# Attention scores and maxima as pairs of 64-row matmuls, and each projection as one run of twelve

## What is computed

```python
q, k, v = (proj(Wq), proj(Wk), proj(Wv))
scores = jnp.einsum('bhqd,bhkd->bhqk', q, k)
bias = rel_bias[_relative_position_buckets(S)]
scores = scores + bias.transpose(2, 0, 1)[None]
attn = jax.nn.softmax(scores, axis=-1)
ctx = jnp.einsum('bhqk,bhkd->bhqd', attn, v)
```

## Time and profile before

| | |
|---|---|
| median of 3 runs | 3967.45 us (3962.96 to 3972.64) |
| span of the profiled execution | 3970.6 us |
| PE busy | 3864.0 us, 97% |
| POOL busy | 2685.8 us, 68% |
| DVE busy | 2459.6 us, 62% |
| ACT busy | 2034.9 us, 51% |
| granted TensorE clock, mean | 0.989 |

### The profile page before, as it was taken

How to read it: one execution, slowest core, us unless ns; L and a number is a source line. 1 busy time by engine, 2 the same in 40 slices (tenths; PEclk the granted TensorE clock), 3 DMA queues, 4 the chain that set the end, 5 groups by cost and what they waited for, 6 DMA issues and landing times. The chain is left out here.

```text
span 3970.6 us, 59813 instructions
## 1 busy us (share of the span) xinstructions
PE 3864.0 (97%) x18973; PEld 2189.4 (55%) x18973; DVE 2459.6 (62%) x3356; ACT 2034.9 (51%) x3452; POOL 2685.8 (68%) x1402
## 2 busy tenths in 40 slices
PE   8999999999999999999999999999997999997899
PEld 7754444444444444444444444444446888885477
DVE  3456666666666666666666666666634777775632
ACT  3335555555555555555555555555543555553232
POOL 1128888888888888888888888888893434430010
PEclk9989999999999999999999999999998999998999
DMA  7642222322222352222332222332312333335710
GB/s 222 168 104 57 62 60 62 94 74 62 62 59 62 93 161 60 64 60 59 87 85 60 64 59 60 88 83 59 100 34 83 107 101 103 106 104 174 278 45 22
DMA packets 395504, 352.29 MB, mean 89 GB/s; under 512 B 193947, under 2 KB 268187, under 8 KB 394008
## 3 DMA queue, kind: packets, MB, share of 16 engines
q1 hardware_dynamic: 326200, 321.84, 28.2%
q10 hardware_dynamic: 67168, 20.98, 2.2%
q0 software_dynamic: 1920, 6.29, 0.5%
HBM read 142.64 MB, written 89.70 MB: 59 GB/s over the span
## 5 line engine op out<-in xcount | busy, mean ns | idle before, releaser
L328 POOL TENSOR_TENSOR acc<-acc,probs 128x1024 f32<-128x1024 f32 x894 | 2127.2, 2379 | 263.5 <-ACT probs L798 138.7
L928 DVE TENSOR_REDUCE maxes<-ps 128x1 f32<-128x1024 f32 x1024 | 1251.2, 1222 | 700.9 <-PE ps L579 696.4
L801 ACT ACTIVATE probs<-ps,far_bias 128x1024 f32<-128x1024 f32 (+7 forms) x1280 | 1022.0, 820 | 1018.5 <-DVE near_s L945 561.2
L614 PE MATMUL ps<-probs,v_head 128*64 128x512 f32 x4096 | 992.2, 605 | 2.1 <-ACT ctx_out L784 2.0
L579 PE MATMUL ps<-stacks 64*128 64x512 f32 x2048 | 751.1, 447 | 16.4 <-issue 7.4
L594 PE MATMUL ps<-stacks 64*128 64x512 f32 x1792 | 662.1, 449 | 0.0
L593 PE MATMUL ps<-stacks 128*128 128x512 f32 x2048 | 619.2, 419 | 0.3 <-ACT probs L798 0.3
L594 PEld LDWEIGHTS ps<-stacks 64*128 64x128 f32 x1792 | 276.9, 185 | 501.0 <-issue 328.4
L614 PEld LDWEIGHTS ps<-probs,v_head 128*64 128x64 f32 x4096 | 248.6, 136 | 483.6 <-issue 481.4
L593 PEld LDWEIGHTS ps<-stacks 128*128 128x128 f32 x2048 | 351.3, 189 | 216.4 <-issue 164.0
L945 DVE TENSOR_TENSOR near_s<-ps,near_bias 128x384 f32<-128x384 f32 (+2 forms) x576 | 284.7, 494 | 268.9 <-PE ps L594 246.1
(11 more groups left out here) (281 smaller groups left out, 4751.7 us busy)
## 6 DMA issues: line engine op xcount, KB each, us to landing
stacks<-c_k SPq DMA_DIRECT2D x128, 256.0 KB, 2.5
stacks<-c_q SPq DMA_DIRECT2D x128, 256.0 KB, 2.6
stacks<-c_d SPq DMA_DIRECT2D x256, 128.0 KB, 2.7
scr_v<-probs ACTq DMA_DIRECT2D x32, 512.0 KB, 4.0
stacks<-c_q SPq DMA_DIRECT2D x128, 128.0 KB, 2.7
v_head<-scr_v SPq DMA_DIRECT2D x32, 512.0 KB, 3.6
scr_ctx<-ctx_out SPq DMA_DIRECT2D x128, 128.0 KB, 2.3
both_ctx<-scr_ctx SPq DMA_DIRECT2D x32, 512.0 KB, 4.0
```

Source lines behind the costliest of these rows:

```text
L328: pool.tensor_tensor(acc[:, qb, :], acc[:, qb, :], pr, ALU.add).then_inc(s["summed"], 1)
L614: mm = pe.matmul(ps[64 * half:64 * half + 64, PV, :], v_head[:, side, kt, :], probs[:, st % PT_RING, half * 512:(half + 1) * 512], start=k ...
L801: ins = act.activation(probs[:, st % PT_RING, a:z], sc[:, a:z], ACT.Exp, bias=bias)
L928: dve.tensor_reduce(maxes[:, qt, pair:pair + 1], ps[:, bank:bank + 2, :], AX.XY, ALU.max).then_inc(s["max_done"], 1)
```

## The change

The 128-row score matmuls go. Every score product becomes a pair of 64-row matmuls, one in each half of the array's rows: the upper lane for the first 512 queries of the half, the lower for the second 512. For that `stacks` is laid out anew: the differences high (`KD`), differences low (`KL`) and keys high (`KH`) stand in both lanes, 64 rows each, and the queries (`QS`) are split between the lanes, high in the left half of the columns, low in the right. A step is three pairs (four where the guard is written, now from small tensors `guard_keys` and `guard_q`). The maxima are pairs too: two query tiles, one in each lane, against the same 512 keys; DVE reduces each to two columns instead of one.

```diff
-PROJ_GROUPS = {4 * tb + 1 + i: (tb, 4 * i, 4 * i + 4) for tb in (0, 2) for i in range(3)}
-PROJ_GROUPS.update({4 * tb + 2 + i: (tb, 6 * i, 6 * i + 6) for tb in (1, 3) for i in range(2)})
+PROJ_GROUPS = {4 * tb + 2: (tb, 0, len(TERMS)) for tb in range(BLOCKS)}
...
-FILLS_MAX, FILLS_SCORE = 16 * 2 * BLOCKS, 16 * (3 * BLOCKS + 1)
+FILLS_MAX, FILLS_SCORE, FILLS_GUARD = 16 * 3 * BLOCKS, 16 * 5 * BLOCKS, 32
...
             def guard(m, side, half):
...
-                sp.dma_start(stacks[0:1, side, QB, half * QW:(half + 1) * QW].bitcast(F32).rearrange("o (t p) -> o t p", p=P),
-                             scr["neg"][half].rearrange("(o p t) -> o t p", o=1, p=P), allow_slow_non_contiguous=True).then_inc(s["neg_in"], 16)
+                for part in range(2):
+                    sp.dma_start(guard_q[guard_row(part, half), :].bitcast(F32).rearrange("o (t p) -> o t p", p=P),
+                                 scr["neg"][half].rearrange("(o p a t) -> a o t p", o=1, p=P, a=2)[part], allow_slow_non_contiguous=True).then_inc(s["neg_in"], 16)
 
             def fill(m, side):
...
-                    sp.dma_start(stacks[:, side, KX, cols].bitcast(F32), c_k[:, cols]).then_inc(s["fill_max"], 16)
-                    sp.dma_start(stacks[:, side, QA, cols].bitcast(F32), c_q[:, cols]).then_inc(s["fill_max"], 16)
+                    for half in range(2):
+                        sp.dma_start(stacks[lane(half), side, KH, cols].bitcast(F32), c_k[0:64, cols]).then_inc(s["fill_max"], 16)
+                    sp.dma_start(stacks[lane(tb % 2), side, QS, q_high].bitcast(F32), c_q[0:64, cols]).then_inc(s["fill_max"], 16)
...
                     for half in range(2):
-                        sp.dma_start(stacks[64 * half:64 * half + 64, side, KA, cols].bitcast(F32), c_d[0:64, own]).then_inc(s["fill_score"], 16)
-                    sp.dma_start(stacks[64:128, side, QB, cols].bitcast(F32), c_q[0:64, cols]).then_inc(s["fill_score"], 16)
-                sp.dma_start(first_keys[64:128, side, :].bitcast(F32), c_k[64:128, 0:LOOKBACK]).then_inc(s["fill_score"], 16)
+                        sp.dma_start(stacks[lane(half), side, KD, cols].bitcast(F32), c_d[0:64, own]).then_inc(s["fill_score"], 16)
+                        sp.dma_start(stacks[lane(half), side, KL, cols].bitcast(F32), c_k[64:128, cols]).then_inc(s["fill_score"], 16)
+                    sp.dma_start(stacks[lane(tb % 2), side, QS, q_low].bitcast(F32), c_q[64:128, cols]).then_inc(s["fill_score"], 16)
...
+                past(pe, s["exped"], n * STEPS + st - 1)
+                if kt < 2:
+                    if kt == 0:
+                        pe.wait_ge(s["neg_in"], FILLS_GUARD * (2 * n + qb + 1))
+                    for half in range(2):
+                        pe.matmul(ps[:, bank + half, :], guard_keys[lane(half), qb, :], guard_q[lane(half), :], start=True, stop=True)
+                for of_keys, of_queries in ((KD, q_high), (KD, q_low), (KL, q_high)):
+                    for half in range(2):
+                        mm = pe.matmul(ps[:, bank + half, :], stacks[lane(half), side, of_keys, keys], stacks[lane(half), side, QS, of_queries],
+                                       start=False, stop=True, skip_group_check=True)
+                mm.then_inc(s["scored"], 1)
...
-                    row_tiles(n, side, g, 0, own, own and not start)
...
+                        scores(n, side, 2 * g)
+                        scores(n, side, 2 * g + 1)
+                    if has_max(n, g):
+                        largest(n, side, g, 1)
                     if prep and g in PROJ_GROUPS:
                         project(n + 2, *PROJ_GROUPS[g])
...
                     if own:
                         exp(n, k, side, 2 * g)
+                        exp(n, k, side, 2 * g + 1)
                     if prep and g in EVAC_GROUPS:
                         take_out(n + 2, EVAC_GROUPS[g])
...
-                    if own:
-                        exp(n, k, side, 2 * g + 1)
...
-                dve.tensor_reduce(maxes[:, qt, pair:pair + 1], ps[:, bank:bank + 2, :], AX.XY, ALU.max).then_inc(s["max_done"], 1)
+                dve.tensor_reduce(maxes[:, qt:qt + HALF_GROUPS // 2 + 1:HALF_GROUPS // 2, first_chunk + pair], ps[:, bank:bank + 2, :], AX.X, ALU.max).then_inc(s["max_done"], 1)
```

More of the change, by code:

```diff
@@ L584, in score @@
-            def score(side, st, half, kind):
+                qt, first_chunk = max_tiles(turn)
+                if late and g == FIRST_MAX and pair == 0:
+                    pe.wait_ge(s["fill_max"], FILLS_MAX * (m + 1))
+                if isinstance(n, int) and n < 0:
+                    past(pe, s["max_done"], 2 * turn + pair - 1)
+                else:
+                    past(pe, s["max_done"], GROUPS * 2 * m + 2 * turn + pair)
+                q = slice((qt // 8 * 4 + qt % 8) * P, (qt // 8 * 4 + qt % 8 + 1) * P)
@@ L586, in score, with scores @@
+                keys = slice((first_chunk + pair) * 512, (first_chunk + pair + 1) * 512)
+                for half in range(2):
+                    mm = pe.matmul(ps[:, max_bank(n, pair) + half, :], stacks[lane(half), mside, QS, q], stacks[lane(half), mside, KH, keys],
+                                   start=True, stop=True)
+                mm.then_inc(s["maxed"], 1)
+            def scores(n, side, st):
                 qb, kt = divmod(st, NT)
                 keys = slice(kt * P, (kt + 1) * P)
-                q = slice(qb * QW + half * 512, qb * QW + half * 512 + 512)
@@ L589, in score @@
-                out = ps[:, SC + 2 * (st % 2) + half, :]
-                if kind == "first":
-                    return pe.matmul(out, first_keys[:, side, keys], stacks[:, side, QB, q], start=True, stop=True)
-                if kind == "high":
-                    return pe.matmul(out, stacks[:, side, KA, keys], stacks[:, side, QA, q], start=False, stop=True, skip_group_check=True)
-                return pe.matmul(out, stacks[64:128, side, KX, keys], stacks[64:128, side, QB, q], start=False, stop=True, skip_group_check=True)
@@ L596, in row_tiles @@
-            def row_tiles(n, side, g, which, own, base):
-                for i in range(2):
-                    if base:
-                        mm = score(side, 2 * g + which, i, "low")
-                    if has_max(n, g):
-                        max_half(n, side, g, which, i)
-                if base and which == 1:
-                    mm.then_inc(s["scored"], 1)
+                q_high = slice(qb * 512, (qb + 1) * 512)
+                q_low = slice(QL + qb * 512, QL + (qb + 1) * 512)
@@ L697, in head @@
                         key_values(0)
-                    row_tiles(n, side, g, 1, own, own and not start)
                     if isinstance(n, int) and n == -1:
@@ L1030, in head @@
                         near(n, k, side, 2 * g)
+                        near(n, k, side, 2 * g + 1)
                     if stepped:
                         step(*stepped)
-                    if own:
-                        near(n, k, side, 2 * g + 1)
                     if has_max(n, g):
```

90 lines of the change are left out of this document (38 added, 52 removed).

## The result

The changed kernel takes 4175.86 us (median; 4169.57 to 4178.93) against 3969.37 for the kernel before on the same chip: a ratio of 1.0515, 95% interval 1.0499 to 1.053. It is slower by 206 us, in the direction forecast and 41 us above the predicted 4135.

The account below looks back on a forecast made before the run. PE bounds the kernel now at 84.9 us a head; afterwards SP's 32-DMA fill delays `take_out`: 25.3 + 65.3 = 90.6 us a head. 30 laps x 5.6 = 168 onto 3967.45 gives 4135 us, range 3990 to 4230.

Parts of the forecast that it names:

- The mechanism: SP's longer fill delays `take_out`, then DVE's `queries_low` and `largest`; PE stops in group 4: 90.6 us a head, chance 0.75.
- The price per DMA: SP's fill: 0.64 us for each DMA whatever its rows, so 32 DMAs take 20.5 us, 7.1 more.
- the last term: From `take_out` to POOL's next division: the later of POOL's 63.0 us and PE's 65.3 with the slow clock.
- the clock: After PE's idle time of 6 us each head, a stretch at 1.2 GHz loses 3.3 us.
- PE's way: PE's work in the lap from `take_out` through step 30 with its exponential and add: 62.0 us without slow clock.
- The gain on PE: PE's list falls from 83.9 to 77.1 us a head, 6.8 gained; with DVE waits PE alone at 80.
- The dear pairs: Every 64-row pair costs 0.34 us, its weight load uncovered: 10 us a head on PE, 4270 us in all; chance 0.09.
- the rival in which the fill keeps its place: SP's fill does not delay `take_out`, so PE gains 1 to 5 us a head: 3820 to 3940 us; chance 0.12.
- The rival "bytes": Fill DMAs cost bytes, not count: fill 13.4 to 15.3 us, 3895 us in the middle; decides below 0.5 per DMA; chance 0.12.

Follow-up runs that it names:

- the narrower wait: Changed kernel, fill still 32 DMAs, but block 0's `take_out` waits only for the maxima's twelve DMAs and its own five score DMAs: 3958.73 us, ratio 0.9966.
- 32 DMAs in the kernel before: Kernel before the change, its fill cut by rows into 32 DMAs in place of 21 for the same bytes, PE's work untouched: 4191.83 us, ratio 1.0559.
- the kernel with the zeros: Changed kernel with 24 matmuls of zeros ahead of the second maxima of group 4, where PE stands still: 4132.92 us, ratio 1.0407.
- with 13: Changed kernel with the same fill bytes in 13 DMAs in place of 32: 4190.09 us, ratio 1.0557.

## Why the prediction came out as it did

**The mechanism held, link by link.** The fill's count makes `take_out` late; DVE's `queries_low` and the reduction behind it follow; PE stops at the second maxima of group 4, at half the clock behind it. The prediction named each of these, and cutting the first link in one kernel and making it in another (the narrower wait, 32 DMAs in the kernel before) took the whole loss away and brought it without the change.

**The price per DMA held, and the fill was still mis-sized.** Its steps are 0.64 us in the median, as reckoned. But in nearly every head one DMA takes 1.0 to 2.2 us in place of 0.60, such as that at 1751.83. Save for one of 24.3 in head 14, the fills of heads 1 to 29 are 20.8 to 22.0 us long, 21.55 in head 16, for the 20.5 of the sum. The lap of head 16, from POOL's division to the next one:

```profile
1733.01 1.28 POOL L319 TENSOR_TENSOR ctx_out<-ctx_out,sums 128x512 f32<-128x512 f32 x1
...
1824.88 1.28 POOL L319 TENSOR_TENSOR ctx_out<-ctx_out,sums 128x512 f32<-128x512 f32 x1
```

Its 91.87 us in the prediction's terms: 2.90 to the first DMA (2.9), 21.55 of fill (20.5), 1.79 of landing and start (1.9), 65.6 from `take_out` to the division (65.3). The fill's 1.05 us and the last term's 0.3, less the 0.1 in between, are some 1.3 a lap, or 38 us on 30 laps, of the miss of 41.

**Two errors in the last term cancel.** Without the clock PE's way was put at 62.0; the kernel with the zeros shows 64.1 (1741.72 to 1805.81). The DVE waits of group 5 (0.70) and group 13 (0.41 and 0.44) were missing, 1.6 of these 2.1; the loop-end idle time is not on this way, since PE resumes at 1805.86, when the division has begun. The clock was put at 3.3, as if PE worked through a whole slow stretch as in head 14 of the kernel before; here the stretch begins while PE still waits, PE loses 2.3 in head 16, and the clock was worth 1.4 a lap. That the sum came out within 0.3 us is luck.

**The gain on PE was over-estimated, which the stall concealed.** A pair costs 0.23 us (1.54 for twelve matmuls and 0.85 for six, at 1782.97, the end of the last one included in both), the groups without projection take 4.12 us (1748.69 to 1752.81) where 4.14 was forecast, and a projection adds 3.0 (7.12 from 1771.16 to 1778.28, for 4.12): all as reckoned. The dear pairs are excluded. The Trainium skill, page "TensorE: Matmul & The Clock Gate", section "The mechanism" of its packing part, lets a weight load overlap a running matmul only in another row group. A run of pairs at 0.23 us each does not agree with that, though it agrees with a sentence ahead of it in the same section, which also lets a load into the background weight buffer go first. But "PE alone would be at 80 us a head" left out 3.1 us of DVE waits at five places and the 1.3 to 1.9 at each second head's end. Without the stall a head takes 84.7 to 84.9 us, as before. So the rival in which the fill keeps its place would have come out near 3960 by the kernel with the narrower wait, about no change, and not at its 3895.

**The rival "bytes" was framed wrongly.** It was to decide below 0.5 us per DMA. Fewer DMAs don't get there: with 13 the count no longer binds, and the transfer takes as long. The two limits lie together, so neither cutting nor merging helped this fill; what helped was to wait for less of it. Two of the rival's numbers are a little off: its bytes were 3.7 and 4.2 MB, which gives 15.0 us and not 15.3, and the middle of its range is 3880. Nothing else hangs on them.

## What to carry to other kernels

When a change saves work on the busiest engine, count what it adds to the transfer queue, and follow the last of it to who waits for all of it; here 11 DMAs cost 217 us, where the change without their stall gains 14. Before shortening such a transfer, ask whether the waiter needs the whole of it: a semaphore for the part that is overwritten cost nothing and was worth 217 us. And of a gain on one engine subtract the partner's time group by group, not on average: DVE waits of 3.1 us a head took back most of what PE saved, and the loop's end nearly all the rest.

## What the runs showed of the hardware that was not expected

**Two limits on a queue that look like one.** In a row, DMAs from 16 to 256 KB took 0.64 us of SP's time each from one start to the next, with median landings of 1.8 to 2.5 us, whether the engines were 59% or 88% busy. Wide 64-row DMAs left at 0.57 at first; with the engines 98% busy at 207 GB/s some held SP for up to 2.5 us.

**One long DMA issue in each fill.** In the changed kernel nearly every fill has one, in the kernel before about every second one (fill lengths of 13.4 and 13.8 to 14.8 us by turns in most heads; the fill of the earlier trace rows is a short one). In the 4 us around that of head 16 (1750 to 1754) the list of DMA queues shows an instruction transfer, and none in the 6 us ahead:

```profile
q8 instruction: 1, 0.02, 2.1%
```

That SP's own program is loaded there, and more often with a longer list, would fit, but no run tried it.

**What lowers the clock, and what it costs.** With PE waits of 4.4 to 8 us came slow stretches of 3.4 to 10.2 us at 0.50, which began before the wait was over; 5.86 us of matmuls with zeros in the same place kept it at 1.00 in head 16 although they compute nothing. The price was 1.6 us there, of the 2.3 that the slowed engine lost.
